# Retention and cross-attention self values by stationary weights and TensorE transposes, in one decoder layer kernel

## What is computed

```python
# retention: 8 heads, key width 128, value width 256
q, k, v, g = x @ Wq, x @ Wk, x @ Wv, x @ Wg          # per head; rope on q, k
scores = einsum("bihd,bjhd->bhij", q * scale, k) * D[None]   # D: causal decay
o = einsum("bhij,bjhd->bihd", scores, v)
o = o * rsqrt(mean(o * o) + EPS) * g_norm_weight * (g * sigmoid(g))
x = _layernorm(x + o @ Wo)
# cross-attention: 16 query heads, 4 key/value heads, width 128,
# keys and values: 722 of the context, then the 100 of x itself
q, k, v = x @ wq, x @ wk, x @ wv                     # rms_norm and rope on q, k
k_ctx, v_ctx = ctx @ wk_ctx, ctx @ wv_ctx
out = softmax(q @ concat(k_ctx, k).T * scale + mask) @ concat(v_ctx, v)
x = _layernorm(x + out @ wo)
x = _layernorm(x + ffn(x))
```

## Time and profile before

| | us |
|---|---|
| median of 3 runs | 3078.92 |
| lowest and highest of them | 3078.42, 3080.01 |
| span of the profiled execution | 3078.5 |
| TensorE busy in it (matmuls) | 2955.7 |
| VectorE, ScalarE busy | 1386.7, 1015.6 |

### The profile page before, as it was taken

One profiled execution on the slowest core, in us unless ns is written; L12 is line 12 of the kernel. 1 busy time (PEld: TensorE's weight loads), 2 busy tenths in 40 slices (PEclk: granted clock), 3 DMA queues, 4 the chain that ended last, 5 costly groups with the idle time before them and its releaser, 6 DMA issues. The chain is left out here.

```text
span 3078.5 us, 42322 instructions
## 1 busy us (share of the span) xinstructions
PE 2955.7 (96%) x16636; PEld 2818.0 (92%) x16636; DVE 1386.7 (45%) x1679; ACT 1015.6 (33%) x1472; POOL 138.9 (5%) x173
## 2 busy tenths in 40 slices
PE   7999999899999999799889999999899999999997
PEld 7899899799999999699879999989699999999996
DVE  3322232344444444788368888833522222222224
ACT  3322322222222222444156766721321221221212
POOL 0000000000000000000022232200000000000000
PEclk9999999999999999999989999999999999999998
DMA  4232232211111111011222112111111111111111
GB/s 165 82 108 77 77 110 86 74 52 55 41 55 41 55 55 41 28 58 62 68 66 63 58 55 65 51 42 55 41 55 62 61 55 68 55 66 57 55 68 56
DMA packets 86924, 195.48 MB, mean 63 GB/s; under 512 B 9232, under 2 KB 64116, under 8 KB 73432
## 3 DMA queue, kind: packets, MB, share of 16 engines
q1 hardware_dynamic: 86872, 194.78, 18.9%
HBM read 164.55 MB, written 30.21 MB: 63 GB/s over the span
## 5 line engine op out<-in xcount | busy, mean ns | idle before, releaser
L113 PE MATMUL PS<-XH,WH 128*128 128x400 f32 x2112 | 739.6, 350 | 34.9 <-DVE XL L549 11.4
L114 PE MATMUL PS<-XL,WH 128*128 128x400 f32 x2112 | 729.5, 345 | 0.0
L115 PE MATMUL PS<-XH,WL 128*128 128x400 f32 x2112 | 727.4, 344 | 0.0
L113 PEld LDWEIGHTS PS<-XH,WH 128*128 128x128 f32 x2112 | 400.3, 190 | 50.1 <-issue 24.4
L114 PEld LDWEIGHTS PS<-XL,WH 128*128 128x128 f32 x2112 | 399.4, 189 | 0.0
L115 PEld LDWEIGHTS PS<-XH,WL 128*128 128x128 f32 x2112 | 399.2, 189 | 0.1
L1664 DVE TENSOR_TENSOR WL<-RAW,WH 128x1024 fp32r<-128x1024 f32 x96 | 117.6, 1225 | 584.2 <-ACT WH L1658 584.2
L83 ACT ACTIVATE WH<-RAW 128x1024 fp32r<-128x1024 f32 x106 | 112.2, 1060 | 647.3 <-PE PS L115 344.0
L89 DVE TENSOR_TENSOR WL<-RAW,WH 128x1024 fp32r<-128x1024 f32 x106 | 129.7, 1224 | 394.5 <-ACT WH L83 393.8
L1658 ACT ACTIVATE WH<-RAW 128x1024 fp32r<-128x1024 f32 x96 | 101.8, 1060 | 597.8 <-PE PS L115 597.8
L389 PE MATMUL PS<-CH,CWH 128*128 128x338 f32 (+1 forms) x512 | 168.1, 328 | 18.8 <-DVE CL L314 18.8
(11 more groups left out here) (202 smaller groups left out, 5478.3 us busy)
## 6 DMA issues: line engine op xcount, KB each, us to landing
RAW<-weights_dram SPq DMA_DIRECT2D x105, 1024.0 KB, 4.8
a_KRAW<-keys_scratch SPq DMA_DIRECT2D x32, 411.0 KB, 3.4
R<-context_dram SPq DMA_DIRECT2D x8, 1536.0 KB, 7.0
a_VRAW<-values_scratch SPq DMA_DIRECT2D x32, 384.0 KB
R<-context_dram SPq DMA_DIRECT2D x8, 1352.0 KB, 6.5
values_scratch<-VS SPq DMA_DIRECT2D x40, 256.0 KB
keys_scratch<-R SPq DMA_DIRECT2D x8, 768.0 KB, 6.2
keys_scratch<-R SPq DMA_DIRECT2D x8, 676.0 KB, 5.5
```

Of the source, the lines that this page charges most:

```text
L113: pe.matmul(out, wh, xh[:, k, cols], start=(k == 0), stop=False)
L114: pe.matmul(out, wh, xl[:, k, cols], start=False, stop=False)
L115: mm = pe.matmul(out, wl, xh[:, k, cols], start=False, stop=(k == KT - 1))
```

## The change

It does four things.

1. `value_matmuls` goes. The values of a retention head are two weight-stationary units, V0 into banks 4, 5 and V1 into banks 6, 7, right behind unit K. ScalarE copies each to SBUF as plain float32 (`VT`, which is the tile `SQ` used later in the head), and `turn_values` transposes it by TensorE, 8 transposes a unit (one for each sequence; the 128x100 tile is stationary, the 128x128 identity `ID` moves, both float32), back into banks 4 to 7 as [100 tokens, 256 outputs]. The high and low part are then made from there as before.
2. The output projection of a loop head stands behind V0 and V1, cut in two: tiles 0 to 3, the 16 transposes, tiles 4 to 7. It now rotates over two bank pairs, 0 and 2, since 4 to 7 hold the values, so that a tile waits for the add of the tile but one before. On VectorE the low part of the values (the new L589) stands between the adds of tiles 3 and 4. The scores come last, ahead of the gate unit, in every head.
3. `phase_self_kv` and its barrier go. `phase_heads` now makes the four value units first, each with eight transposes behind the next unit, then the four key heads, then the sixteen query heads. ScalarE copies a value unit to SBUF, VectorE copies the transposed one to its place at the end of `QX`, and SyncE issues the stores of values and keys between the weight loads. VectorE waits for all of them ahead of the last two turns, which write where the values stood.
4. In `phase_attention` GpSimd no longer waits for the stores, and the heads are found at other offsets. The order of the packed weights follows.

The diff, cut to its core:

```diff
@@ -116,22 +117,13 @@
     mm.then_inc(c.unit_done, 1)
-def value_matmuls(c, pe, sweep, bank):
-    wh = c.WH[:, sweep, :].rearrange("p (k n) -> p k n", n=256)
-    wl = c.WL[:, sweep, :].rearrange("p (k n) -> p k n", n=256)
+def turn_values(c, pe, src, bank, offset, stride):
     for b in range(B):
-        out = c.PS[0:T, bank + b // 2, (b % 2) * 256:(b % 2 + 1) * 256]
...
+        at = offset + b * stride
+        mm = pe.transpose(c.PS[0:T, bank + at // 512, at % 512:at % 512 + P],
+                          src[:, b * T:(b + 1) * T], c.ID[:])
+    return mm
 def rsqrt_from(c, act, out, stat, eps, ln_done, ln_count):
...
@@ -453,26 +445,22 @@
+        WV, WO, WG = 2, 4, 6
+        WO_BANKS = [(0, 2)[n % 2] for n in range(KT)]
+        VT = SQ
         def unit_no(unit, i, first):
...
@@ -504,21 +492,20 @@
                         weights_ahead(n, i, first)
                         act.wait_ge(roped, 2 * i + (n + 1))
                         act.activation(QK[n][0][:], T1[:], ACT.Copy).then_inc(qk_hi, 1)
+                    for t in range(2):
+                        weights_ahead(WV + t, i, first)
+                        act.activation(halves(VT[:, t, :]), banks2(c, 4 + 2 * t),
+                                       ACT.Copy).then_inc(v_kept, 1)
                     if not first:
                         weights_ahead(WO, i, first)
+                    act.wait_ge(v_turned, i + 1)
+                    act.activation(VH[:].rearrange("p (g b) n -> p g (b n)", b=2),
+                                   c.PS[0:T, 4:8, :], ACT.Copy).then_inc(v_hi, 1)
+                    if not first:
                         weights_ahead(WO + 1, i, first)
-                    def scores():
...
+                    act.wait_ge(s_masked, i + 1)
+                    act.activation(SH[:], SM[:], ACT.Copy).then_inc(s_hi, 1)
                     weights_ahead(WG, i, first)
                     act.activation(halves(G[:, 0, :]), banks2(c, 2), ACT.Silu).then_inc(gated, 1)
...
@@ -591,40 +578,33 @@
                 def head(i, first):
                     rope(0, i, first, lambda: weights_ahead(0, i, first))
-                    def while_k_is_split():
...
+                    rope(1, i, first, lambda: weights_ahead(1, i, first))
+                    for t in range(2):
+                        weights_ahead(WV + t, i, first)
                     if not first:
-                        for n in range(1, KT):
+                        for n in range(4):
                             add_output(n, i)
-                            if n % 4 == 3:
...
+                        weights_ahead(WO, i, first)
+                    dve.wait_ge(v_hi, i + 1)
+                    dve.tensor_tensor(VL[:].rearrange("p (g b) n -> p g (b n)", b=2),
+                                      c.PS[0:T, 4:8, :],
+                                      VH[:].bitcast(F32).rearrange("p (g b) n -> p g (b n)", b=2),
+                                      ALU.subtract).then_inc(v_lo, 1)
+                    if not first:
+                        for n in range(4, KT):
...
@@ -670,19 +650,19 @@
                     else:
                         pe.wait_ge(c.w_lo, 8 * i + (U_RET - 2 + unit + 1))
-                def project_output(i, last):
-                    for n in range(KT):
+                def project_output(i, last, tiles):
+                    for n in tiles:
                         if n % 4 == 0:
-                            pe.wait_ge(c.w_lo, 8 * i + (U_RET + (n // 4 + 1) - (2 if last else 0)))
+                            pe.wait_ge(c.w_lo, 8 * i + (U_RET + (n // 4 + (-1 if last else 3))))
                         if n == 0:
                             pe.wait_ge(o_lo, 2 * i)
-                        if n >= 3:
...
+                        if n >= 2:
+                            pe.wait_ge(r_added, 8 * i + (n - 1 - 8))
+                        elif not last:
+                            pe.wait_ge(roped, 2 * i + (n + 1))
                         for h in range(2):
...
@@ -710,31 +690,36 @@
                         pe.wait_ge(o_ln, i)
                     unit_matmuls(c, pe, 1, 2, XH, XL)
                     if not first:
-                        project_output(i, False)
...
+                        pe.wait_ge(o_gated, i)
+                    for t in range(2):
+                        weights(WV + t, i, first)
+                        unit_matmuls(c, pe, t, 4 + 2 * t, XH, XL)
+                    if not first:
+                        project_output(i, False, range(4))
+                    pe.wait_ge(v_kept, 2 * i + 2)
+                    for t in range(2):
+                        mm = turn_values(c, pe, VT[:, t, :], 4, t * P, RDV)
+                    mm.then_inc(v_turned, 1)
+                    if not first:
+                        project_output(i, False, range(4, KT))
+                    pe.wait_ge(qk_lo, 2 * i + 2)
+                    if not first:
+                        pe.wait_ge(r_added, 8 * i - 1)
+                    for b in range(B):
+                        out = c.PS[0:T, b // 4, (b % 4) * T:(b % 4 + 1) * T]
+                        cols = slice(b * T, (b + 1) * T)
+                        (qh, ql), (kh, kl) = QK
+                        pe.matmul(out, kh[:, cols], qh[:, cols], start=True, stop=False)
+                        pe.matmul(out, kh[:, cols], ql[:, cols], start=False, stop=False)
+                        mm = pe.matmul(out, kl[:, cols], qh[:, cols], start=False, stop=True)
+                    mm.then_inc(s_raw, 1)
+                    if not first:
+                        pe.wait_ge(r_added, 8 * i)
                     weights(WG, i, first)
                     unit_matmuls(c, pe, 0, 2, XH, XL)
...
@@ -944,6 +929,11 @@
         squared, sq_hi, sq_lo, taken, var, ln, rs, roped, out = (sem(n) for n in (
             "squared", "sq_hi", "sq_lo", "taken", "var", "ln", "rs", "roped", "out"))
+        v_kept, v_turned, v_copied = sem("v_kept"), sem("v_turned"), sem("v_copied")
+        stored = c.kv_stored
+        VF = c.QX[:, 12 * NT:14 * NT].rearrange("p (s n) -> p s n", s=2)
+        VT = c.QX[0:T, 20 * NT - KV_N * B * HD:20 * NT].rearrange("p (v b d) -> p v b d", v=KV_N, b=B)
@@ -959,7 +949,24 @@
             @block.sync
             def _(sp):
-                weight_stream(c, sp, U_QK // 2 + 2, HEADS // 4)
+                weight_stream(c, sp, U_V // 2 + 2, 2)
+                for v in range(KV_N):
+                    sp.wait_ge(v_copied, v + 1)
+                    for lo, hi, chunk, row in ((0, P - SELF_P, SELF_C, SELF_P),
+                                               (P - SELF_P, T, SELF_C + 1, 0)):
+                        sp.dma_start(
+                            c.vscr[:, v, row:row + hi - lo, chunk, :].rearrange("b p d -> p b d"),
+                            VT[lo:hi, v, :, :]).then_inc(stored, 16)
+                weight_stream(c, sp, U_V // 2 + 6, 1)
+                for v in range(KV_N):
+                    sp.wait_ge(out, 2 + v + 1)
+                    sp.dma_start(c.kscr[:, v, :, CTX:KEYS].rearrange("b p t -> p b t"),
+                                 c.QX[:, v * NT:(v + 1) * NT]
+                                 .rearrange("p (b t) -> p b t", t=T)).then_inc(stored, 16)
+                weight_stream(c, sp, U_V // 2 + 8, 3)
+                sp.wait_ge(stored, 16 * KV_STORES)
+                sp.dma_start(c.KRAW[:], c.kscr[0, 0]).then_inc(c.k_in, 16)
             @block.tensor
             def _(pe):
@@ -974,15 +981,39 @@
                         mm = pe.matmul(bank, ONE[:], SQL[:, cols], start=False, stop=True)
                     mm.then_inc(var, 1)
+                def turned(v):
+                    pe.wait_ge(v_kept, v + 1)
+                    if v >= 2:
+                        pe.wait_ge(v_copied, v - 1)
+                    turn_values(c, pe, VF[:, v % 2, :], 4 + 2 * (v % 2), 0,
+                                HD).then_inc(v_turned, 1)
                 norm.tensor(pe)
+                for v in range(KV_N):
+                    if v >= 2:
+                        pe.wait_ge(v_kept, v - 1)
+                    pe.wait_ge(c.w_lo, U_V + v + 1)
+                    unit_matmuls(c, pe, v % 2, 2 * (v % 2), c.XH, c.XL,
+                                 (lambda h, k: norm.wait_inputs(pe, h, k)) if v == 0 else None)
+                    if v > 0:
+                        turned(v - 1)
                 def turn(i, first):
                     for j in range(4):
                         pe.wait_ge(taken, 4 * i + (j + 1))
+                        if first and j < 2:
+                            pe.wait_ge(v_kept, j + 3)
                         pe.wait_ge(c.w_lo, 4 * i + (U_QK + j + 1))
-                        unit_matmuls(c, pe, j % 2, 2 * (j % 2), c.XH, c.XL,
-                                     (lambda h, k: norm.wait_inputs(pe, h, k))
-                                     if j == 0 else None)
+                        unit_matmuls(c, pe, j % 2, 2 * (j % 2), c.XH, c.XL)
+                        if first and j == 0:
```

(14 more changed lines are left out.)

## The result

| | before | after |
|---|---|---|
| median, us | 3079.47 (3078.42 to 3082.76, 4 runs) | 3033.13 (3032.48 to 3034.00, 4 runs) |
| span of the profiled execution, us | 3078.5 | 3032.2 |
| ratio of the times | | 0.9849, 95% interval 0.9835 to 0.9863 |

The changed kernel is 1.5% faster. The forecast was 3031 us, within a range of 3023 to 3055.

A forecast was written before the change was run, and what follows sets the result against it. TensorE bounds retention's loop and the heads, a chain of waits the stretch from last head to attention. Gains 21.4 + 1.5 + 24.8 = 47.7 us; 3078.5 - 47.7 + 0.4 = 3031 us, range 3023 to 3055.

The forecast's parts named there:

- The values of a loop head: Retention's loop: two weight-stationary units, 17.50 us, replace 192 matmuls of 22.66 us, a gain of 5.16 us a head.
- The price of a transpose: TensorE's transposes of the values: 0.10 us each, taken from the scores' row; 16 a head cost 1.6 us (1.4 to 3.4).
- (a): Rival on the transposes: float32's two records, 0.213 us each, 18.1 us more, 3049 us; chance 22%.
- (b): Rival on the transposes: they don't overlap, each takes a whole 0.252 us, 24.3 us more, 3055 us; chance 8%.
- The wait at tile 6: Loop head's output projection: TensorE waits 0.9 us for VectorE's add of tile 4, which follows the values' low part.
- The 0.4 us of old waits: Loop head's eight output tiles: 0.4 us of waiting for adds behind K's low part goes, with V0 and V1 ahead.
- Waits costed at nothing: Loop head: other new waits (V1's copy, adds of tiles 0 to 3, weight splits) are covered and cost nothing.
- (c): Rival in retention's loop: V1's copy, adds or a weight split lag some 2 us in seven heads, 14 us, 3045; chance 6%.
- The first head: Retention's first head: no output tiles cover V1's split and copy, 2.0 us stand open; gain 1.5 us.
- The last projection: Retention's last output projection, with two bank pairs instead of three: tile 6 is tightest; 0 to 1 us of cost.
- Cross-attention: Last head to attention: 65.9 us today, less 38.2 for values made ahead and 2.9 for barrier and prologue; gain 24.8 us.
- attention's start: Attention's first stretch, at a granted clock of 0.58, was to stay as it was, with no gain there.

## Why the prediction was right

**The result** lies 2 us above the forecast, and a part of that closeness is luck. The prediction has attention 47.7 us earlier; it is 43.6 earlier. The missing 4.1 us are 2.3 in the loop, 0.5 in the first head, 0.2 in the last projection, 0.6 in cross-attention and 0.5 by which retention starts later. The 2.7 us that came back lie behind attention's first matmul, where the prediction has no gain.

- **The values of a loop head.** Forecast: two units in 17.50 us for 22.66. Units Q, K, V0 and V1 take 35.02, which is 8.755 each: right.
- **The price of a transpose.** Forecast 0.10 from the scores' row, against 0.213 for two records; measured 0.104 by the stage and 0.109 in full, 1.5 us in 160. The run with ordinary matmuls shows both that (a)'s price exists and that the transpose doesn't pay it. This was the choice on which 18 us hung, and the reason given for it, no second record, is what the traces show. (b) falls with it: a record lasts 0.273 us, more than the 0.252 it was priced at, but they overlap.
- **The wait at tile 6.** Place, releaser and mechanism were right. The stop itself, for which the prediction's rows give 5.3 - 4.4 = 0.9 us, measures 0.97: tile 6 starts 1.15 us after the matmul ahead of it, 769.50 to 770.65, instead of 0.18. To it comes a restart that the prediction left out: the next matmul stands 0.29 behind tile 6's first (770.94) and not 0.18. Together this is nearly 1.1 us, and the kernel without the wait is 1.05 a head shorter. The rest of the 1.19 by the stages (9.92 - 8.73) is the transposes' 0.1 from above. With 0.17 for the wait and 0.15 for sixteen transposes (1.75 for 1.60) seven heads lose 2.2 us, nearly all of the loop's 2.3 (19.1 for 21.4).
- **The 0.4 us of old waits** in the output tiles were to go, and did: tiles 0 to 3 take 8.73 us, which is 48 x 0.182.
- **Waits costed at nothing.** In TensorE's table of waits for the loop there is none but tile 6's and the one on G of the earlier trace rows. Right, and rival (c) falls, though the 1.1 us a head of tile 6 were of its kind: (c) needed 2.
- **The first head.** Forecast 1.5, measured 1.0, with the expected wait ahead of the transposes, 1.93 us of idle time released by ScalarE's copy. Of the missing 0.5, 0.15 are the transposes. The rest is about what the clock cost: over the first 5 us of the head the granted clock is 0.63 before and 0.56 after, 0.7 us more at the low level, half of it lost. Nothing ties that to the change.
- **The last projection.** 0.2 us more, within the 0 to 1.
- **Cross-attention.** 24.2 for 24.8; half of the difference are the 32 transposes, 3.5 us for 3.2. From the last finish to attention 2.79 us for 2.9. That the stores hide was right: SyncE issues the eight from 1327.25 on and is through 22.7 us later, where the prediction had 17, and no load comes late, since TensorE is busy for 155.00 of 155 us there:

```profile
1327.25 22.74 SPq L957 DMA_DIRECT2D values_scratch<-QX  x8
1350.10 14.61 SPq L71 DMA_DIRECT2D RAW<-weights_dram  x2
1364.91 7.57 SPq L964 DMA_DIRECT2D keys_scratch<-QX  x4
```

  The step "a gap of 17.5 us, in which SyncE issues stores" is wrong if it is read as a cause. The sum took the gap away whole, so it did not suffer; but a reader who had wanted to save the gap alone would have put the stores on two queues and gained nothing, where cutting 46 rows into 32 and 14 gains 6.8 us.
- **Not foreseen:** attention's start. It was to stay as in the earlier trace rows; it is 1.5 us shorter, since the full clock comes 9.1 us after the first matmul (1510.15 to 1519.28) instead of 12.0 (1553.75 to 1565.78). This may be luck too: five more kernels here reach attention with the same 5.75 us of idle time, and their clock takes from 8.8 to 11.9 us (last section). The last 1.2 us lie in later phases that the change does not touch, and are left unexplained.

## What to carry to other kernels

Where tokens fill only 100 of 128 stationary columns, weights stationary and a TensorE transpose behind cost less (here 17.5 and 1.75 us for 22.66), if the transposes are written in that form and stand in a closed row of matmuls, where only the distance of their starts counts. When an engine's order is redone, ask of each long elementwise step what now stands behind it: here one move on VectorE was worth 7 us. And before a wait for stores is put down to the queue that issues them, look at the share of DMA engines that is busy, for a DMA's speed can hang on its number of rows.

## What the runs showed of the hardware that was not expected

- A float32 matmul of 128 moving columns, 100 stationary, costs 0.218 us in a row and appears as two records; the transpose of the same shape costs 0.109 us in one. For the pair of forms this is a factor of 2.0.
- Two stores of 46 rows (184 KB) and two of 54 (216 KB) moved at 43 GB/s with a tenth of the DMA engines busy and, in bursts, at 160; with each 46 cut into 32 and 14 the long stretches at 43 were gone. SyncE's issue of a store took 2.1 us at the mean for the four and 0.6 for the six that replaced them.
- The time from attention's first matmul to the first one whose record is shortened by the full clock was 12.0 us before, 11.9 with two queues and 10.1 in retention's half alone (1532.90 to 1543.04), with 17.5 to 17.9 us of idle TensorE ahead; 11.4 with the cut stores, with 11.4 us ahead; and with 5.75 us ahead 9.1 after, 9.1 in cross-attention's half alone, 9.1 and 9.8 with the late low part (9.8 with the scores first), 8.8 with ordinary matmuls and 11.9 with four times the transposes (1561.01 to 1572.87). Kernels with the same idle time differ by up to 3.1 us, so the idle time alone does not set it; what does is open.
